# Attention with a causal power-law mask and an fp4 feed-forward: the mask of own blocks on VectorE, plain pairs for VectorE, and new orders of work

## What is computed

```
xn   = layernorm(x)                                   # 2048 x 128
q,k,v= split(xn @ w_attn + b_attn), 16 heads of 8
s    = q k^T * 8**-0.5 + mask                          # per head 2048 x 2048
mask = -log(1 + key - query) where key > query, 0 where equal, -inf where key < query
attn = softmax(s) @ v ;  out_a = attn @ w_proj + b_proj
ffn  = fp4(silu(fp4(xn) @ fp4(w_gate)^T) * (fp4(xn) @ fp4(w_up)^T)) @ fp4(w_down)^T
fp4  : per block of 16 values, scale = max|.|/6, round to {0,.5,1,1.5,2,3,4,6}
```

## Time and profile before

| | |
|---|---|
| median of 3 runs | 598.94 us (597.7 to 599.84) |
| the profiled execution, its own time | 599.36 us |
| its span, first to last instruction | 597.6 us |
| TensorE (PE) busy | 562.5 us, 94% |
| VectorE (DVE) busy | 547.1 us, 92% |
| ScalarE (ACT) busy | 409.3 us, 68% |
| GpSimd (POOL) busy | 503.2 us, 84% |
| granted TensorE clock, mean | 0.997 |

### The profile page before, as it was taken

The page is one execution under the profiler, slowest core; times in us unless marked ns, Lnnn a source line. Parts: engine busy times, 40 slices in busy tenths (PEclk is TensorE's granted clock), DMA queues, the critical chain, the costliest instruction groups (busy, mean ns, idle before and its releaser), DMA issues.

```text
span 597.6 us, 11270 instructions
## 1 busy us (share of the span) xinstructions
PE 562.5 (94%) x3791; PEld 247.5 (41%) x3791; DVE 547.1 (92%) x1165; ACT 409.3 (68%) x868; POOL 503.2 (84%) x409
## 2 busy tenths in 40 slices
PE   5999999999899999999999999999999998999995
PEld 4677844544343434333333333342344343343322
DVE  5999989998999899999999999999998989999672
ACT  4668486675665567766776676767666767677793
POOL 7378888797998889798999989897988889798773
PEclk9999999999998999999999999999999999999999
DMA  7434344010000001000000000000000000000000
GB/s 203 103 104 113 110 99 108 2 74 8 1 3 1 2 1 60 39 1 2 1 1 1 20 1 2 1 2 2 1 2 19 2 0 2 2 0 2 2 2 18
DMA packets 14832, 16.66 MB, mean 28 GB/s; under 512 B 1639, under 2 KB 14216, under 8 KB 14360
## 3 DMA queue, kind: packets, MB, share of 16 engines
q1 hardware_dynamic: 14240, 15.70, 9.5%
q10 hardware_dynamic: 536, 0.26, 0.2%
HBM read 11.75 MB, written 4.01 MB: 26 GB/s over the span
## 4 chain that ended last, share of the span: by engine, by line
PE 53%; DVE 27%; issue 7%; ACT 7%; POOL 5%; POOLq 0%; ACTq 0%; DVEq 0%
PE psum L1467 14%; DVE mxp L1240 13%; PE psum L1425 13%; PE psum L1449 10%; DVE ring L1267 4%; PE psum L1310 3%; POOL ring L895 3%; PE psum L1381 2%; ACT ring L1049 2%; PE psum L1400 2%; PE psum L1428 2%; PE psum L1383 1%; PE psum L1452 1%; DVE psum L1222 1%; DVE xw L1218 1%
## 5 line engine op out<-in xcount | busy, mean ns | idle before, releaser
L895 POOL TENSOR_TENSOR ring<-ring,dist 128x1024 f32<-128x1024 f32 (+3 forms) x223 | 398.6, 1815 | 51.6 <-ACT ring L1049 50.8
L1240 DVE TENSOR_REDUCE mxp<-psum 128x1 f32<-128x512 f32 (+3 forms) x640 | 354.7, 598 | 16.6 <-PE psum L1425 13.9
L1049 ACT ACTIVATE ring<-psum 128x512 f32<-128x512 f32 (+3 forms) x446 | 221.8, 557 | 93.5 <-PE psum L1452 46.8
L1425 PE MATMUL psum<-kop,qop 96*128 96x512 bf16 (+3 forms) x640 | 198.4, 352 | 7.2 <-DVE mxp L1240 3.7
L1449 PE MATMUL psum<-qop,kop 128*128 128x512 bf16 (+3 forms) x640 | 191.2, 349 | 7.4 <-DVE mxp L1240 2.8
L1467 PE MATMUL psum<-ring,vaug 128*32 128x512 f32 (+3 forms) x1280 | 155.3, 556 | 2.5 <-POOL ring L895 1.9
L1267 DVE TENSOR_TENSOR ring<-psum,dist 128x512 f32<-128x512 f32 (+3 forms) x194 | 115.1, 620 | 12.0 <-ACT psum L1049 11.4
L1049 ACT ACTIVATE psum<-psum 128x512 f32<-128x512 f32 (+3 forms) x194 | 99.7, 545 | 31.7 <-PE psum L1449 19.0
L1425 PEld LDWEIGHTS psum<-kop,qop 96*128 96x128 bf16 x640 | 56.5, 97 | 134.6 <-DVE mxp L1240 45.5
L1449 PEld LDWEIGHTS psum<-qop,kop 128*128 128x128 bf16 x640 | 59.3, 97 | 83.6 <-DVE mxp L1240 19.7
L1428 PE MATMUL psum<-tri_q,identb 128*128 128x128 bf16 x256 | 55.9, 220 | 0.0
(11 more groups left out here) (134 smaller groups left out, 467.9 us busy)
## 6 DMA issues: line engine op xcount, KB each, us to landing
parts_dram<-qpart SPq DMA_DIRECT2D x18, 128.0 KB, 3.4
kop<-parts_dram SPq DMA_DIRECT2D x6, 384.0 KB
qop<-parts_dram SPq DMA_DIRECT2D x6, 384.0 KB
xin<-_attn_hidden_states_dram SPq DMA_DIRECT2D x4, 256.0 KB, 5.0
ring<-inv_dram SPq DMA_DIRECT2D x1, 1024.0 KB, 5.1
out_dram<-xin SPq DMA_DIRECT2D x4, 256.0 KB, 2.3
qop<-parts_dram SPq DMA_DIRECT2D x3, 288.0 KB
kop<-parts_dram SPq DMA_DIRECT2D x3, 288.0 KB
```

The source lines that it names most:

```text
L895: g_.tensor_tensor(slot(p)[:, 0:n], slot(p)[:, 0:n], both, ALU.mult).then_inc(weighed_pool, 1)
L1049: a_.activation(scores if pair_vec[p] else slot(p)[:, 0:n, e % 2], scores, ACT.Exp, scale=SCALE).then_inc(exp_done, 1)
L1240: v_.tensor_reduce(mxp[:, u % 2, 4 * a + j, c - g:c - g + 1], bank(*o)[:, 0:n], AX_X, ALU.max).then_inc(max_used, 1)
L1425: ins = mm(bank(*o)[:, 0:n], qop[0:K_MAX, u // NQ % 2, h, P * a:P * (a + 1)], kop[0:K_MAX, h, k0:k0 + n], start=True, stop=(c != g))
```

## The change

It has four parts.

1. **The mask.** The list of reciprocals is zero where the distance is below 1, that is where the key is ahead of the query. Two small VectorE instructions make this at the start. For own blocks of a pair that VectorE weighs, TensorE leaves out the triangle, and VectorE takes the minimum with 3e38 before it multiplies (SCALAR_TENSOR_TENSOR in place of TENSOR_TENSOR), so that an exponential that overflowed gives zero as well. Own blocks of GpSimd pairs keep the triangle.
2. **The slot of a VectorE pair** holds head 0's elements and then head 1's. VectorE writes, and TensorE reads, without a stride. GpSimd pairs stay interleaved.
3. **The price of a GpSimd pair in the plan** goes from 220 + 2.04 per element to 140 + 1.906 per element: 2092 ns in place of 2309 for a pair of full heads (1024 elements). Some items change place and some pairs change engine.
4. A limit of its own for own blocks, `OWN_QUEUE`, which has the same value as `POOL_QUEUE`.

```diff
-POOL_COL, POOL_START = 2.04, 220
+POOL_COL, POOL_START = 1.906, 140
...
+                own = steps[e // 4][1] < TPG * (units[steps[e // 4][0]][0] + 1)
-                pair_vec[p] = behind > (LAST_QUEUE if work["max"] == total else POOL_QUEUE)
+                pair_vec[p] = behind > (LAST_QUEUE if work["max"] == total else OWN_QUEUE if own else POOL_QUEUE)
...
+        def weighted(p, j, n):
+
+            if pair_vec[p]:
+                return slot(p).rearrange("p n j -> p (n j)")[:, GQ * j:GQ * j + n]
+            return slot(p)[:, 0:n, j]
...
+                seq(v_.tensor_scalar(valid[:], invd[:], 0.0, 1.0, ALU.max, ALU.min))
                 seq(v_.tensor_scalar(invd[:], invd[:], 1.0, None, ALU.max))
-                v_.reciprocal(invd[:], invd[:]).then_inc(inv_ready, 1)
+                seq(v_.reciprocal(invd[:], invd[:]))
+                v_.tensor_tensor(invd[:], invd[:], valid[:], ALU.mult).then_inc(inv_ready, 1)
...
-                    v_.tensor_tensor(slot(p)[:, 0:n, e % 2], bank("st", e)[:, 0:n], weights(d, n),
-                                     ALU.mult).then_inc(weighed_vec, 1)
+                    if d < TPG:
+                        v_.scalar_tensor_tensor(out=weighted(p, e % 2, n), in0=bank("st", e)[:, 0:n], scalar=FINITE,
+                                                in1=weights(d, n), op0=ALU.min, op1=ALU.mult).then_inc(weighed_vec, 1)
+                    else:
+                        v_.tensor_tensor(weighted(p, e % 2, n), bank("st", e)[:, 0:n], weights(d, n),
+                                         ALU.mult).then_inc(weighed_vec, 1)
...
-                             qop[0:K_ST, u // NQ % 2, h, 0:n], start=True, stop=(d >= TPG))
-                    if d < TPG:
+                             qop[0:K_ST, u // NQ % 2, h, 0:n], start=True, stop=(d >= TPG or pair_vec[e // 2]))
+                    if d < TPG and not pair_vec[e // 2]:
...
-                                 slot(2 * s + j // 2)[:, 0:n, j % 2], start=(b == NT - 1), stop=(b == TPG * g))
+                                 weighted(2 * s + j // 2, j % 2, n), start=(b == NT - 1), stop=(b == TPG * g))
```

More of the change, by code:

```diff
@@ L42 @@
 NEG = -1e30
+FINITE = 3e38
 EPS = 1e-5
@@ L62 @@
 POOL_QUEUE, LAST_QUEUE = 3800, 1500
+OWN_QUEUE = 3800
 MROWS = 3
@@ L499, in build @@
         invd = sb("invd", [P, S // P + 1], F32)
+        valid = sb("valid", [P, S // P + 1], F32)
         vaug = sb("vaug", [P, NT, VC * NH + 32 - VC], F32)
@@ L1048, in _ @@
                         act.wait_ge(pv_done, (p - SLOTS) // 2 + 1)
-                    a_.activation(scores if pair_vec[p] else slot(p)[:, 0:n, e % 2], scores,
+                    a_.activation(scores if pair_vec[p] else weighted(p, e % 2, n), scores,
                                   ACT.Exp, scale=SCALE).then_inc(exp_done, 1)
```

## The result

The changed kernel takes 601.49 us (median of 5 runs, 601.21 to 602.35), the kernel before 598.94. The ratio is 1.0041, 95% interval 1.0021 to 1.0061: 2.5 us slower. The forecast was 595.2 us, in a range up to 603.5. The profiled execution of the changed kernel took 601.41 us, its span is 599.6 us against 597.6.

The account below looks back on a forecast made before the run. VectorE was taken to lead up to the last join with TensorE close behind, ScalarE in the tail. Span 597.6 - 21.5 (join) + 17.7 (tail) = 593.8 us; against the median, 595.2 us, range 588.5 to 603.5.

Parts of the forecast that it names:

- The join: The point where VectorE joins the last unit's maxima, 552.75 us before; forecast 21.5 us earlier, near 531 us.
- the two bounds: Limits on the join's gain: 17.7 us earlier if TensorE alone sets the pace, 25.3 if VectorE alone does.
- GpSimd's busy time ahead of the join: GpSimd weighs 214 pairs there in place of 208, and wider ones: 10.6 us more work.
- The tail grows: Behind the last join 99 heads remain in place of 69; at ScalarE's rate, with feed-forward instructions, 17.7 us more.
- GpSimd keeps up with ScalarE: Last unit: 13 GpSimd pairs in place of 11, 23 us of work, about what ScalarE needs; nothing added.
- the closing steps may end a microsecond later or earlier: End of the kernel: GpSimd no longer rests, so the end may shift by a microsecond; nothing added.
- VectorE alone: Rival: VectorE alone sets the pace, join 25.3 us earlier, span 591.3 us; chance 0.08.
- TensorE sets the pace: Rival: join 17.7 us earlier, the tail takes all of it back, 598.9 us, no change; chance 0.20.
- GpSimd as the bound: Rival: GpSimd limited to 93.2% busy, 415.8 us of work, join 14.2 us earlier, 602.4 us; chance 0.25.
- The signs: Join near 531 us, tail near 62; wrong if the join is later than 535 us or the tail over 66.
- Mask and stride: Fewer triangles on TensorE and slots without stride: taken at nothing beyond the join's sum; stride rival's chance 0.02.
- The cover at the start: Mask instructions delay VectorE by some 0.45 us; 0.46 us before TensorE's first product hides it, so nothing.

Follow-up runs that it names:

- r17: Kernel before, with early TensorE waits filled by zero products and constant turns, and late waits filled by constant turns: 598.30 us, ratio 0.9988.
- r14: Changed kernel, with early TensorE waits filled by zero products and constant turns, and late waits filled by constant turns: 599.03 us, ratio 1.0008.
- r3: Changed kernel, with TensorE turning a constant into free banks in its last waits: 601.11 us, ratio 1.0029.
- r13: Kernel before, with only the early TensorE waits filled (44 products of zeros, then 12 and 6 turns of a constant): 598.40 us, ratio 0.9991.
- r10: Changed kernel with maxima running further ahead (SOON, SOON_MORE 40, 24; queue limits 4400), 79 VectorE pairs: 601.02 us, ratio 1.0042.
- r15: r10 with TensorE's early and late waits filled: 598.80 us, ratio 1.0007 to the kernel before.
- r5: Changed kernel with TensorE adding the triangle to all own blocks again (256 in place of 194): 601.42 us, ratio 1.0046 to the kernel before.
- r4: Changed kernel with VectorE's pairs interleaved (strided) in their slots as before: 601.89 us, ratio 1.0045 to the kernel before.
- r18: Changed kernel's mask and plain slots on the old price's order, with TensorE's early and late waits filled: 598.90 us, ratio 1.0003 to the kernel before.
- r2: Kernel before with the new GpSimd pair price alone, old mask and slots: 601.35 us, ratio 1.0045.
- r7: Changed kernel with 36 small products of zeros on TensorE from 1.07 us on: 601.12 us, ratio 1.0032 to the kernel before.
- r8: Changed kernel with the old GpSimd price, 36 early zero products and constant turns in TensorE's last waits: 600.06 us, ratio 1.0019 to the kernel before.

## Why the prediction was wrong

**The join.** "21.5 us earlier" measured 20.3 (552.75 to 532.46), inside the two bounds and 1.2 short. But the trace of the kernel before has the fall of the clock at 191 us in it; with the clock held (r17, r14) it is 18.8, 2.7 short, and nearer to the bound for TensorE alone (17.7). GpSimd's busy time ahead of the join was over-estimated: 3.7 us more (475.3 to 479.0), not 10.6. The sum left out that GpSimd's three instructions of one feed-forward tile, 0.94, 0.93 and 0.79 us, fall behind the join as well.

**The tail grows, "17.7 us more".** This is the step that failed. From the join to the last copy it is 20.5 us more, 2.8 over the sum. ScalarE's own work in it was nearly right: 18.4 us more (8.41 + 21.07 before, 28.02 + 19.86 now). It grew by 31 full heads and by three instructions that the sum left out, the copy of unit 13's sum (0.63 us) and the two of the feed-forward's tile 14 (0.42 and 0.30), but a head took rather less than 0.55 us of it where ScalarE did not wait (four in 2.01 us at 549.51): its records overlap by over 0.1 us, more than the 40 to 80 ns given ahead of the prediction.

What the sum put at nothing is the waiting: ScalarE is idle for 9.0 us between join and last copy, 6.9 before, 2.1 us of the 2.8. Of that 1.3 us is in the last unit, where it has three full heads fewer than before and the unit takes 24.4 us all the same. There "GpSimd keeps up with ScalarE" and "I add nothing" failed: GpSimd is busy for 21.4 us of the unit, 19.2 before, and the last two steps with v wait 1.34 us for its pairs. No run tells GpSimd's part in the idle time from the rest. Join and tail together: the join lost 1.2 and the tail 2.8, so the gain of 3.8 us was gone; with the clock held they lost 2.7 us each (r17 and r14).

```profile
533.17 0.63 ACT L1084 ACTIVATE osb<-psum 128x512 f32<-128x512 f32 x1
...
538.21 0.42 ACT L1042 ACTIVATE hT<-psum 128x256 f32<-128x256 f32 x1
538.47 0.30 ACT L1045 ACTIVATE hT<-psum 96x128 f32<-96x128 f32 x1
```

**What was not in the sum at all:** the clock at the end, 1.8 us (8.3 to 10.1). The prediction wrote that "the closing steps may end a microsecond later or earlier" because GpSimd no longer rests, and added nothing. The price was not in the idle time but in the rate of the matmuls behind it. r3 shows that the clock stays up when the waits are filled; that GpSimd's pairs brought the fall is not shown (r13 has it without them). And the clock had cost the profiled kernel before something too: in its trace it fell at 191 us for 3.4 us, and the trace's span is 1.0 to 2.0 us over those of the group at 595.6 to 596.6. By the spans with a held clock (r17, r13 and r14) order, mask and slots cost 1 to 1.5 us, in place of a gain of 3.8.

**The rivals.** TensorE or VectorE alone had the join at 17.7 and 25.3 us earlier; it lay between. With the clock held the outcome is that of "TensorE sets the pace": a join 18.8 us earlier, a tail that takes it back, no change clear of noise. No run tests TensorE as the cause. GpSimd as the bound had 93.2% busy, a join 14.2 us earlier and 602.4 us. The time was near that, 601.5, and GpSimd's share was 93.4%, but the way was another: with 410.7 us of work in place of 415.8 the join was nearly on time. Nor is 93.2% a bound: in r10 GpSimd is busy for 410.7 of the 430.5 us from 92.9 us to the join, 95.4%. In the changed kernel its waits for exponentials fell from 50.8 to 32.4 us, and TensorE's for its pairs rose:

```profile
POOL ring L905 <- ACT ring L1059: 32.4, 33, 3.0
...
PE psum L1483 <- POOL ring L905: 11.3, 22, 1.3
```

So GpSimd did come onto the path (27% of the chain that ended last, 5% before), but its load alone did not decide the loss: r10 and r15 put five pairs more on it and are no slower than the changed kernel and r14.

```profile
PE 53%; POOL 27%; ACT 9%; DVE 6%; issue 4%; ACTq 0%; POOLq 0%; DVEq 0%
```

**The signs.** Of those given for being wrong two came true: the tail is 67.1 us, over 66, and TensorE's waits for GpSimd's pairs grew; the join was not later than 535 us. The others held or nearly: 535.8 us of VectorE and 526.6 of GpSimd for 532 and 530, 194 triangles, 32.4 us of GpSimd's waits, 681 ns a full head.

**Mask and stride** were taken at nothing. r5 and r4 agree for triangles and stride, and by r4 the estimate from the Trainium skill's Vector Engine (DVE) Microarchitecture Reference, § Measured stream behaviour on trn2, some 50 us of VectorE's work, is not there at a stride of two (681 and 685 ns). The cover at the start (0.46 us over 0.45) held nearly: TensorE's first transposes ran from 8.79 us, 8.73 before. It is gone where TensorE is already fast: 8.79 us in r18, 8.58 in r17.

**How sure it was.** The gain forecast was the difference of two numbers near 20 us, each good to one or two; the chance of 0.55 for faster was too high for a difference of 3.8. The measured time lies in the range only because the range took in the rival of GpSimd as the bound, whose way it did not go.

## What to carry to other kernels

When a change moves work off an engine in one phase, ask which engine takes it in the next, and price that phase from every instruction that moves and from the waits it had before; a join that comes 20 us earlier is worth nothing where ScalarE then stands alone with the rest. A plan's right price need not give a better order: here it moved the last copy by only 0.2 us, to later. And in a kernel this full a few waits of one microsecond on TensorE near the start or the end can cost 1 to 2 us by the clock, more than the edit under test.

## What the runs showed of the hardware

- The times of one kernel fall in groups about 1.9 us apart. Executions at full recorded clock are parted by the start: the same four records of the first product with the weights took 1.96 us or 3.54 to 3.75 us, with a recorded clock of 1.00 in both, and with TensorE busy from 1.1 us on the upper group is gone (r13 to r18). That the clock has not yet come up there is read from the durations.
- In the changed kernel the clock fell at 590.2 us, with waits of 1.34 and 0.81 us on TensorE ahead of the fall; with turns of a constant in the waits it stayed up to 597.7 and 596.7 us (r3, r14). In r13 it fell at 590.3 us behind waits of only 0.21 and 0.80 us, near the end of one of 0.77. Where it falls differs between executions: in r2, r4, r5 and r7 at 592.5 to 594.5 us.
- More work early is not enough: with a wait of 1.48 us behind it the clock fell again at 10.8 us (r7), though with one of 1.49 us it did not in r8's profile.
- A stride of two f32 words costs VectorE's writes nothing (681 and 685 ns for 512 columns) and TensorE's reads nothing that these runs can show (621 and 623 ns a record of 512 columns).
- A full GpSimd pair takes 2.14 us whether VectorE is 92% or 89% busy beside it. GpSimd was busy for 95.4% of 430 us in r10, so 93% was no limit of it.
